# Softmax row sums divided out on VectorE head by head, instead of by turned inverse sums on TensorE

## The reference, cut to what matters

```python
h = concat([x, latents], axis=1)                  # 375 + 112 = 487 keys
q = (latents @ q_w + q_b).reshape(b, 112, 16, 32)
k, v = split(h @ kv_w + kv_b)                     # 16 heads of 32
attn = einsum('bkhd,bnhd->bhkn', q, k) / 32
attn = where(full_mask, attn, -inf)
attn = softmax(attn, axis=-1)
attn_out = einsum('bhkn,bnhd->bkhd', attn, v).reshape(b, 112, 512)
attn_out = attn_out @ out_w + out_b + residual
out = gelu(rmsnorm(attn_out) @ mlp_w1 + mlp_b1) @ mlp_w2 + mlp_b2 + residual
```

## Time and profile before

| what | value |
|---|---|
| median of 3 runs | 1054.22 us (1051.39 to 1055.66) |
| profiled execution | 1056.6 us, span 1054.9 us |
| mean granted TensorE clock | 0.945 |
| PE / PEld busy | 927.1 us (88%) / 712.2 us (68%) |
| DVE / ACT / POOL busy | 601.9 us (57%) / 423.8 us (40%) / 225.1 us (21%) |
| L1558, the turned inverse sums, 514 to 875 us | 32 matmul records per sequence |
| L757, the masked maxima | 78.6 us, 128 of 660 ns |
| L1106, the exponentials | 88.4 us, 128 of 692 ns |

### The profile page before, as it was taken

How to read it: one execution, slowest core, us unless ns; L and a number is a source line. 1 busy time by engine, 2 the same in 40 slices (tenths; PEclk the granted TensorE clock), 3 DMA queues, 4 the chain that set the end, 5 groups by cost and what they waited for, 6 DMA issues and landing times.

```text
span 1054.9 us, 17599 instructions
## 1 busy us (share of the span) xinstructions
PE 927.1 (88%) x6888; PEld 712.2 (68%) x6888; DVE 601.9 (57%) x1298; ACT 423.8 (40%) x957; POOL 225.1 (21%) x231
## 2 busy tenths in 40 slices
PE   4765879888888888799699999999999986999998
PEld 4654656565656666466487878778787655788886
DVE  2567989898988898954223323423333244445543
ACT  4113132323222233344365666556566564233332
POOL 2527353535444445200000000000000002000100
PEclk9887898999898989899899999999999988999999
DMA  5463253525353523120600110101010310000101
GB/s 225 142 193 119 69 133 89 133 81 137 96 139 78 146 76 107 53 63 1 230 8 14 42 47 8 48 8 54 11 45 9 161 54 1 0 0 27 44 0 36
DMA packets 35051, 77.11 MB, mean 73 GB/s; under 512 B 12638, under 2 KB 18782, under 8 KB 33567
## 3 DMA queue, kind: packets, MB, share of 16 engines
q1 hardware_dynamic: 34974, 76.07, 24.2%
HBM read 68.72 MB, written 7.34 MB: 72 GB/s over the span
## 4 chain that ended last, share of the span: by engine, by line
PE 50%; issue 24%; POOL 15%; DMA 5%; DVE 3%; ACT 2%; SPq 0%; POOLq 0%; DVEq 0%; ACTq 0%
POOL scan L455 10%; PE bank L1597 9%; PE bank L1473 8%; PE bank L1585 7%; PE bank L1467 6%; PE bank L1488 4%; PE bank L1548 4%; PE bank L1540 3%; POOL xj L446 3%; PE bank L1570 3%; PE bank L1239 2%; DMA scan<-v_scratch 2%; PE bank L1502 2%; POOL scan L458 2%; DMA v_scratch<-vt 1%
## 5 line engine op out<-in xcount | busy, mean ns | idle before, releaser
L757 DVE CUSTOM_DVE_ANT_0 smb<-bank,mask 112x487 f32<-112x487 f32 x128 | 78.6, 660 | 117.7 <-issue 117.6
L565 DVE TENSOR_TENSOR_SCAN scan<-bank,scan 128x448 f32<-128x448 f32 x128 | 132.0, 1073 | 10.0 <-POOL scan L458 10.0
L1239 PE MATMUL bank<-xj,front 128*128 128x112 f32 x1024 | 123.7, 282 | 11.7 <-POOL xj L446 11.7
L1239 PEld LDWEIGHTS bank<-xj,front 128*128 128x128 f32 x1024 | 121.1, 199 | 14.1 <-POOL xj L446 9.0
L455 POOL TENSOR_TENSOR scan<-scan,ks 128x896 f32<-128x896 f32 x64 | 125.8, 1965 | 19.7 <-DMA scan<-v_scratch 19.6
L1106 ACT ACTIVATE smb<-smb,nmax 112x487 f32<-112x487 f32 x128 | 88.4, 692 | 91.9 <-DVE nmax L757 91.9
L432 POOL TENSOR_TENSOR small<-small,neghalf 112x1 f32<-112x1 f32 x24 | 14.3, 597 | 475.9 <-DVE small L781 312.7
L1548 PE MATMUL bank<-ident,smb 112*122 112x112 f32 x512 | 60.8, 268 | 14.6 <-ACT smb L1106 13.6
L572 DVE TENSOR_TENSOR scan<-scan,bank 128x896 f32<-128x896 f32 x64 | 69.3, 1083 | 3.1 <-DVE scan L565 0.5
L1548 PEld LDWEIGHTS bank<-ident,smb 112*122 112x122 f32 x512 | 52.7, 142 | 23.2 <-ACT smb L1106 20.2
L446 POOL TENSOR_TENSOR xj<-tmp,xa 128x448 f32<-128x448 f32 x40 | 41.6, 1057 | 92.9 <-DVE tmp L534 92.9
(11 more groups left out here) (180 smaller groups left out, 1942.5 us busy)
## 6 DMA issues: line engine op xcount, KB each, us to landing
scan<-v_scratch SPq DMA_DIRECT2D x64, 448.0 KB
w<-in_w SPq DMA_DIRECT2D x2, 4096.0 KB, 12.9
cx<-in_ctxt SPq DMA_DIRECT2D x8, 750.0 KB, 5.1
raw_w<-in_wbig SPq DMA_DIRECT2D x4, 1024.0 KB, 13.6
tail<-in_wbig SPq DMA_DIRECT2D x1, 3072.0 KB
front<-in_wbig SPq DMA_DIRECT2D x2, 1024.0 KB, 9.3
x_f<-in_x SPq DMA_DIRECT2D x8, 224.0 KB, 2.9
v_scratch<-vt SPq DMA_DIRECT2D x32, 56.0 KB, 1.8
```

The source lines that it names most:

```text
L565: n = v.tensor_tensor_scan(flat, decay, flat, 0.0, ALU.mult, ALU.add)
L757: v.tensor_tensor_reduce(sm[r], bank[r][0:T, 0:NKEY], mask_b[b % 2][:, :], -1.0 / DH, 3e38, ALU.add, ALU.min, nmax[:, h:h + 1]).then_inc(s ...
L1239: i = t_.matmul(tiles(dst)[:, m, :], w[:, k, m * P:(m + 1) * P], x[:, k, :], start=k == 0, stop=k == NT - 1)
```

## The change

The division moves from the output to the probabilities. `inverse_sums`, `sums_turned`, `keep_inverse` and `attention_output` are gone. In their place VectorE's `normalised(b, k)`, right behind the four maxima of each group, takes for each head the reciprocal of its one column of sums and multiplies the head's 112x487 exponentials by it in place. The turns wait for `normed` instead of `probs`. ScalarE's `attention_high` and VectorE's `attention_low` read the weighted output straight from bank 4, and the buffer `lt` is no longer needed; `attention_low` now stands ahead of all of k=0's maxima. `weighted(b, 0)` waits for `lt_ready` of the sequence before instead of `ao_ready`, and the wait of `scores(b, 0)` for `ri_kept` is gone.

```diff
-            def inverse_sums(b):
-                dve.wait_ge(s["probs"], b * NH + NH)
-                v.reciprocal(rsum[:, 1, :], rsum[:, 0, :]).then_inc(s["rinv"], 1)
-
-            def attention_output(b):
-                dve.wait_ge(s["ri_kept"], b + 1)
-                dve.wait_ge(s["pvh"], b * NT + NT)
-                v.tensor_tensor(lt[:, :, :], tiles(4), lt[:, :, :], ALU.mult).then_inc(s["ao_ready"], 1)
+            def normalised(b, k):
+                for r in range(HG):
+                    h = k * HG + r
+                    dve.wait_ge(s["probs"], b * NH + h + 1)
+                    v.reciprocal(rsum[:, 1, h:h + 1], rsum[:, 0, h:h + 1]).then_inc(s["rinv"], 1)
+                    dve.wait_ge(s["rinv"], b * NH + h + 1)
+                    v.tensor_scalar(sm[r], sm[r], rsum[:, 1, h:h + 1], None, ALU.mult).then_inc(s["normed"], 1)
 
             def attention_low(b):
                 dve.wait_ge(s["lt_hi_ready"], b + 1)
-                v.tensor_tensor(lt_lo[:, :, :], lt[:, :, :], lt_hi[:, :, :].bitcast(F32), ALU.subtract
+                v.tensor_tensor(lt_lo[:, :, :], tiles(4), lt_hi[:, :, :].bitcast(F32), ALU.subtract
                                 ).then_inc(s["lt_ready"], 1)
...
             def attention(b):
                 if b:
-                    attention_output(b - 1)
-                group_max(b, 0, 0, 1)
-                if b:
                     attention_low(b - 1)
-                group_max(b, 0, 1)
+                group_max(b, 0)
+                normalised(b, 0)
                 group_max(b, 1)
+                normalised(b, 1)
...
                 group_max(b, 2)
+                normalised(b, 2)
...
                 group_max(b, 3)
-                inverse_sums(b)
+                normalised(b, 3)
...
-            attention_output(B - 1)
             attention_low(B - 1)
...
-            def keep_inverse(b):
-                act.wait_ge(s["ri_ready"], b + 1)
+            def attention_high(b):
+                act.wait_ge(s["pvh"], b * NT + NT)
                 wait(act, "op_ready", b)
-                c_.copy(lt[:, :, :], tiles(0)).then_inc(s["ri_kept"], 1)
-
-            def attention_high(b):
-                act.wait_ge(s["ao_ready"], b + 1)
-                c_.copy(lt_hi[:, :, :], lt[:, :, :]).then_inc(s["lt_hi_ready"], 1)
+                c_.copy(lt_hi[:, :, :], tiles(4)).then_inc(s["lt_hi_ready"], 1)
...
-                keep_inverse(b)
...
-                    wait(pe, "ri_kept", b)
...
             def probs_turned(b, k):
                 for r in range(HG):
-                    pe.wait_ge(s["probs"], b * NH + k * HG + r + 1)
+                    pe.wait_ge(s["normed"], b * NH + k * HG + r + 1)
...
-            def sums_turned(b):
-                pe.wait_ge(s["rinv"], b + 1)
-                pe.wait_ge(s["pt_kept"], b * NH + NH - HG + 1)
-                for k in range(NT):
-                    for r in range(HG):
-                        p, h = r * DH, k * HG + r
-                        i = t_.matmul(tiles(0)[p:p + DH, k, :], rsum[:, 1, h:h + 1].broadcast_to([T, DH]),
-                                      ident[0:T, 0:T], start=True, stop=True)
-                i.then_inc(s["ri_ready"], 1)
-
             def weighted(b, k):
                 pe.wait_ge(s["pt_kept"], b * NH + (k + 1) * HG)
                 if k == 0:
-                    wait(pe, "ao_ready", b)
+                    wait(pe, "lt_ready", b)
                     pe.wait_ge(s["ffg"], B)
...
-                sums_turned(b)
                 weighted(b, 3)
 
             for b in range(B):
                 attention(b)
-            pe.wait_ge(s["ri_kept"], B)
+            pe.wait_ge(s["pt_kept"], B * NH)
```

More of the change, by code:

```diff
@@ L181, in build @@
         lt_at = room_f.at
-        lt = room_f.take("lt", [P, NT, T])
-        lt_lo = view("lt_lo", lt_at, [P, NT, T], F32R)
+        lt_lo = room_f.take("lt_lo", [P, NT, T], F32R)
         kt[1] = room_s.take("kt1", [P, NT, NKEY])
@@ L242, in build @@
             wsplit_hi wsplit cx_loaded0 cx_loaded1 cx_hi_ready cx_ready kv_ready kv_kept qp_ready qt_ready
-            mask_loaded0 mask_loaded1 mask_eq pad_ready s_done masked probs pt_ready pt_kept pvh rinv ri_ready ri_kept
-            ao_ready lt_hi_ready lt_ready op_ready lat_back latob_ready x1_ready ve3 rstd3 x1n_ready h1T_ready h1_ready
+            mask_loaded0 mask_loaded1 mask_eq pad_ready s_done masked probs pt_ready pt_kept pvh rinv normed
+            lt_hi_ready lt_ready op_ready lat_back latob_ready x1_ready ve3 rstd3 x1n_ready h1T_ready h1_ready
             w1_loaded w2_loaded b1_loaded b2_loaded lat_back0 lat_back1 lat_back2 lat_back3 latb2_ready hp_ready
```

## The result

The changed kernel takes 1074.83 us (median of 4 runs, 1073.98 to 1076.42) against 1054.74 us before (4 runs, 1051.39 to 1055.66): a ratio of 1.0196 with a 95% interval of 1.0165 to 1.0227. It is slower by 20 us, where 1073 was forecast in a range of 1064 to 1088. The profiled execution took 1074.62 us, with a span of 1072.9.

The account below looks back on a forecast made before the run. TensorE, busy 46.15 of 46.33 us a sequence, was taken as the bound. Sequences 1 to 6 add 11.9, sequence 0 2.7 and sequence 7 4.1: +18.7 us, forecast 1073, range 1064 to 1088.

Parts of the forecast that it names:

- The product removed: TensorE's product of turned inverse sums goes: -0.90 us in each of sequences 0 to 6, nothing in sequence 7.
- Off the path: VectorE's old reciprocal and multiply, ScalarE's inverse copy, and the high and low part at a sequence's start: costed at zero.
- The durations: VectorE per head: reciprocal 0.16 us, multiply 0.47, gap 0.03, overlap 0.08, so a pitch of 0.58.
- one element a cycle: Rival, VectorE's multiply: 660 ns, pitch 0.77, +18 on the sum, 1091 us; chance 6%.
- a short pitch: Rival, VectorE's heads: pitch below 0.44 gives no measurable change (6%), below 0.33 a faster kernel (3%).
- The fourth turn: Sequences 1 to 6, TensorE waits for the fourth normalised head: +0.76, +1.13, +0.99 us in k=0 to 2, k=3 covered.
- One sign: TensorE idle before the turns, put down to VectorE: about 1 us in each of k=0, 1, 2, none in k=3.
- What is queued behind: VectorE's residual sum and norm behind k=1's heads move by 2.32 us; nobody waits, by 0.8.
- Sequence 0: Attention stage, sequence 0: k=0 +1.52, then +1.13, +0.99 and -0.90, together +2.7 us.
- Sequence 7: No key/value products there: k=0 +0.76, k=1 +2.32 from the late norm, k=2 and k=3 0.5 each, together +4.1 us.
- The port's held multiply: Rival: one 1510 ns tensor_scalar in each of six sequences, 1.02 us each, +6, 1079 us; chance 5%, inside the range.
- The clock: Rival: TensorE's clock falls once in each of sequences 1 to 6, +10, 1083 us; in all 18 groups +31, 1104; 14%.

Follow-up runs that it names:

- the two kernels with the norm moved: Changed kernel with split cover, old division in sequence 7 and reordered reciprocals, and kernel before with split, both with residual sum and norm moved: 1045.49 and 1048.63 us.
- the kernel without the division: Changed kernel without reciprocals and multiplies, turns waiting for the exponentials, probabilities left undivided: 1045.95 us, ratio 0.9925.
- the pipelined order: Changed kernel with each group's reciprocals issued ahead, so a multiply seldom waits for the instruction just before it: 1069.35 us, ratio 1.0161.
- the best version without the turned product: Changed kernel with split cover, old division in sequence 7 and reordered reciprocals: 1049.85 us, ratio 0.9961; with the norm moved too, 1045.49 us, 0.9926.
- the second kernel: Changed kernel with each multiply after its head's turn, turns waiting for the exponentials alone, turned probabilities undivided: 1057.19 us, ratio 1.0039.

## Why the prediction was right

**The product removed.** Forecast -0.90 a sequence; k=3 fell by 0.92, and the two kernels with the norm moved differ by 0.91. In sequence 7 it was worth nothing, as argued.

**Off the path.** The operations taken away from VectorE and ScalarE, and the high and low part at the start of a sequence, were costed at nothing. That is right: the kernel without the division has the new order, and its k=0 is all TensorE work. One reason given was misread. The prediction has both engines idle for 7 us ahead of the old multiply; the earlier trace rows says so of VectorE, but ScalarE was idle for 0.97 ahead of its part. The cost did not hang on it.

**The durations.** The reciprocal was forecast at 0.16 and took 156 ns (median of 128), the multiply at 0.47 and took 473 ns, the gap and the overlap were 0.04 and 0.08 on average, and the pitch is 0.58. The rivals of one element a cycle (pitch 0.77) and of a short pitch fall with it. That pitch is the term with leverage: the pipelined order started the fourth multiply 0.33 sooner, and 0.34 to 0.37 came off each of k=0, 1 and 2.

**The fourth turn.** Forecast +0.76, +1.13, +0.99 and 0, measured +0.78, +1.14, +1.00 and, with the product gone, -0.92. The sum of +1.98 stands against +1.94 to +2.03 in sequences 1 to 5. The experiment that proves the mechanism is the split: the same work on every engine, with half a cover product moved in front of the turns, and the cost of k=0 and k=2 is gone; that of k=1 goes when the norm is moved as well. One sign came out in kind but not in size: TensorE was to idle about 1 us before the turns of each of these groups, and its matmul rows have 0.49, 0.33 and 0.19, its weight loads 1.47, 1.32 and 1.20.

**What is queued behind.** The residual and norm had 0.8 us to spare in k=1 by the forecast. The rows have 675.32+0.48 = 675.80 against the product's user, which started without a wait at 676.44: 0.64. The step was right for the changed kernel, and it was the next bound as soon as the turns' wait was taken away.

**Sequence 0.** Forecast +2.7, measured +3.10. k=0 grew by 1.92 instead of 1.52; k=1 to 3 as the others. The granted clock was at its lower level until about 520 us in both kernels; in the window 518 to 520 its mean was 0.71 before and 0.59 after, which goes the right way, but no run isolates it. In three other kernels with the changed kernel's code up to there, this k=0 took 10.68, 11.00 and 11.12 us instead of 10.24, the last two with a multiply stretched to 1.30 and 1.44 us by GpSimd's addition. So this term was met only as closely as it repeats.

**Sequence 7.** Forecast +4.1 as 0.76, 2.32, 0.5 and 0.5; measured +4.30 as 0.63, 1.74, 1.19 and 0.74. The lateness of the norm is right: from k=1's first maximum to `mlp_input` it was 853.56-846.71 = 6.85 before, and is 9.16 now, +2.31, ahead of this row:

```profile
870.42 0.61 PE L1225 MATMUL bank<-ident,rows_y 112*128 112x112 f32 x4 [2.84 <-DVE rows_y L784]
```

That k=1 shows only 1.74 of it and k=2 0.69 more than its term was not taken apart further; the clock changes inside this sequence (mean 0.88). The same code took 45.15 us in the split kernel, 0.7 more in k=0 and 0.6 more in k=1. That the sum of four terms came within 0.2 us is in part luck. For k=2 and k=3 the value of 0.5 was a choice below a bound of 1.25, and 1.19 says that the bound was nearer.

**The rivals inside the range.** The port's held multiply was given 5% at one in each of six sequences. It happened once in the changed kernel, at +0.83 of the +20.1. The clock did not fall in sequences 1 to 6 of it. Summed: 11.9 forecast and 11.9 measured in sequences 1 to 6 without the held multiply, then +0.83, +3.10 and +4.30. The stage grew by 1.4 us more than the 18.7 forecast; the profiled span grew by 18.0 only, because the part ahead of the stage was 1.9 shorter.

## What to carry to other kernels

When work is put between two engines' steps, its price is the time by which the last item of a group comes later, read as start plus pitch times heads, and the busy share of the engine that does it says nothing: here a VectorE with half its time free cost a full TensorE 2 us a sequence. Such a latency is paid with order rather than with speed: half a cover product in front of the turns gave back 19.0 of 20.1 us of the stage, where a shorter pitch gave back 6.5 (one execution each). Then look at once at what else stands in the delayed engine's queue, because it is the next wait; with that moved too, the best version without the turned product went from 0.9961 to 0.9926 of the kernel before. Give the old version the same care before you compare: it reached 0.9940, whole runs do not tell the two apart, and what speaks for the moved division is 0.91 us a sequence in the traces.

## What the runs showed of the hardware

A VectorE multiply with one tensor input (112x487 fp32 in SBUF, 0.47 us) and a GpSimd addition (112x512 fp32, 1.30 us alone) did not run side by side. If GpSimd's began first, or both within 0.02 us, the multiply took up to 1.56 us and ended 0.26 to 0.29 after it, in nine kernels. If a multiply was already under way, the addition took the longer the more was left of it: 1.32 us with 0.20 left and 1.53 with 0.40 left (the changed kernel, sequences 0 and 6), 1.57 with 0.41 left (the second kernel, sequence 0). The masked maxima, which read two tensors, one of them in PSUM, kept their 0.66 beside the same addition. The 1510 ns row fits the same reading: it began at 886.21, while GpSimd's timeline of the kernel before has this:

```profile
886.01 4.05 POOL L498 TENSOR_TENSOR lat_all<-lat_all,ob_rows 112x512 f32<-112x512 f32 x2
```

There the row holds two additions. The changed kernel has the same pair by itself: the addition from 903.95 to 905.38, the multiply from 904.15 to 905.67, 1.52 us.

The Trainium skill, "SBUF — State Buffer", section "SBUF: two separate sides", describes such a lock between a GpSimd operation and a VectorE operation that uses both of its ports: whichever starts first holds the shared pair of ports for its whole instruction, and the other blocks. The traces agree, with the 0.27 us on top; which ports the multiply uses they do not show.
